# Second-layer experts: all shared blocks first, pairs weighted by ScalarE and summed by TensorE

## The chip, the cores and the metric

The kernel runs on one core of a Trainium2 chip. The metric is the device time of one execution in microseconds (us); the profile is one execution of it, taken by the hardware profiler.

## What is computed

A two-layer network on x of shape 8 x 512 x 128 (float32), with a mixer and a mixture of experts in each layer. The change lies in the last of the four, the experts of the second layer:

```python
xt = x.reshape(-1, D)                                   # 4096 rows of 128
scores = jax.nn.softmax(xt @ gate_w.T, axis=-1)
idx = jax.lax.top_k(scores + gate_b, 2)[1]              # 2 of 8 experts
weights = jnp.take_along_axis(scores, idx, axis=-1)
cw = jnp.sum(jax.nn.one_hot(idx, E) * weights[..., None], axis=1)
h1 = jnp.einsum('td,efd->etf', xt, w1) + b1[:, None, :]
h3 = jnp.einsum('td,efd->etf', xt, w3) + b3[:, None, :]
y = jnp.einsum('etf,edf->etd', swiglu(h1 * h3), w2) + b2[:, None, :]
routed = jnp.einsum('te,etd->td', cw, y)
shared = swiglu((xt @ sw1.T + sb1) * (xt @ sw3.T + sb3)) @ sw2.T + sb2
return routed + shared
```

`swiglu` takes even and odd columns (gate g and lin l), clips them, and gives g * sigmoid(1.702 g) * (l + 1). The result is scaled by `gb` and added to x.

## The kernel before

`program` runs the stages one after another: `prologue`, `scan_phase`, `experts0`, the attention functions, and `experts1` (L1272), which starts near 1500 us with its layer norm and router and works on experts from 1556 us to the end.

**Blocks.** 4096 rows are 32 tiles of 128 (NT). The shared expert works on 16 blocks of 256 rows (SLOTS) taken straight from `hT`. The routed rows are 8192 pairs of row and expert; they are sorted by expert in two parts (PARTS) of 16 tiles each, each part in 23 blocks (RB) of 256 slots, and every block belongs to one expert. VectorE works out where each pair goes (`pos`, L1531 to L1573) and the expert of each block (`eid`, L1580).

**POOL** then issues, with nothing else to do, 64 indirect DMAs that scatter normalized rows to `sorted_h` in HBM (L1440, 32 for each part). For each part it waits until all 23 blocks' results are stored (L1447) and issues 32 indirect DMAs that gather two rows for each row into `got` (L1449); NGOT = 8 semaphores let it run eight tiles ahead.

**SP** loads, for routed block m, 256 rows from `sorted_h` into one of four buffers (`load_slots`, L1400) and 320 KB of weights of the expert `eid[m]`, whose number it reads into a register (`load_weights`, L1391 and L1392), into one of five, and stores y (`store`, L1406). Its loop issues in iteration m: rows of m+1, weights of m, the store of m-5.

**The order of blocks** is a list, ORDER: 11 shared, 46 routed, 5 shared. For block n TensorE turns the rows of block n+1 if it is routed (L1704), does four matmuls of 256 columns (L1717 to L1726: gate and lin products), and the down product of block n-2 (L1741), for a shared block together with the second biases of all nine experts, weighted by `cwT` (L1740). ScalarE adds the first biases (`gate` L1473, `lin` L1479), does tanh (L1485), and copies turned rows (L1467) and y (L1496). VectorE multiplies and clips (L1600 to L1611) and joins (L1617, L1623).

A routed block's first biases are those of its expert. VectorE selects them for all 46 blocks at once in `select_biases`, ahead of its work on block 4.

**Combining.** `acc` holds the shared result of each tile. `combine(k)` adds two gathered rows, each times its weight, with one VectorE operation each that waits for the one before (L1629). Eight tiles of part 0 are combined inside the block loop, every second block, the other 24 after it; `finish(j)` multiplies four tiles by `gb` and adds x (L1635, L1637), and SP stores them (L1421).

## Time and profile before

| | us |
|---|---|
| median of 3 runs | 1889.8 (1887.2 to 1894.68) |
| the profiled execution's own time | 1888.83 |
| its span in the trace | 1887.1 |
| TensorE matmul busy in the span | 1487.2 (79%) |
| VectorE busy | 1326.4 (70%) |
| ScalarE busy | 908.8 (48%) |
| POOL busy | 612.6 (32%) |

In rows of the trace PE is TensorE's matmuls, PEld its weight loads, DVE VectorE, ACT ScalarE, SPq SyncE's queue. A row of the timeline has start, length, engine, line, operation, output and inputs, count, and in brackets the engine's idle time before it and what ended that. "remote" or "another core or an unknown queue" is a semaphore whose writer the trace doesn't tell, "issue" idle time without a visible wait. PEclk is the granted TensorE clock (0.50 is 1.2 GHz, 1.00 is 2.4 GHz). A `pz` is one of the eight PSUM banks; times count from the start of the span.

### The profile page before, as it was taken

To read this page: it belongs to the slowest core of one execution; us is meant where nothing else is said; L and a number is where in the kernel's file an instruction comes from. 1 tells how busy PE (TensorE), PEld (TensorE's weight loads), DVE (VectorE), ACT (ScalarE), POOL (GpSimd) and SP (SyncE) were. 2 spreads that over 40 slices of the span, in tenths; PEclk is the share of its full clock that TensorE was granted. 3 is DMA by queue.
4 is the path that set the end of the run, shared out by engine and by line. 5 is a ranking of instruction groups with operands and counts; after the bars stand their busy time and mean duration, and the time that the engine had idled before them with its cause. 6 is when DMAs were issued, how large, how long until landed. Compare 5 with 4: busy or idle time off the path is not lost. (4 is left out here: it accounts for less than half of the span.)

```text
span 1887.1 us, 41774 instructions
## 1 busy us (share of the span) xinstructions
PE 1487.2 (79%) x15118; PEld 1007.2 (53%) x15118; DVE 1326.4 (70%) x3609; ACT 908.8 (48%) x2099; POOL 612.6 (32%) x586
## 2 busy tenths in 40 slices
PE   1277777767699399999999999999999395298490
PEld 0177766766554245555555555555555363187370
DVE  6699999999559636666666666666666674177385
ACT  1455555555121226666666666666666122065250
POOL 3496666662103325111111111111110317502414
PEclk7688888888789799999999999999999777599695
DMA  1400000000000012111111111111110001258342
GB/s 68 118 12 1 1 1 1 1 1 1 12 1 1 17 17 35 28 29 29 28 29 30 29 29 30 29 30 30 30 25 8 15 1 56 65 150 224 94 135 78
DMA packets 146373, 71.54 MB, mean 38 GB/s; under 512 B 95218, under 2 KB 131588, under 8 KB 146052
## 3 DMA queue, kind: packets, MB, share of 16 engines
q1 hardware_dynamic: 141508, 60.62, 14.6%
q0 software_dynamic: 4096, 8.40, 1.5%
q8 instruction: 107, 1.75, 0.4%
q14 instruction: 86, 0.70, 0.1%
q10 hardware_dynamic: 576, 0.07, 0.0%
HBM read 38.11 MB, written 18.35 MB: 30 GB/s over the span
## 5 line engine op out<-in xcount | busy, mean ns | idle before, releaser
L1190 DVE TENSOR_REDUCE ntop<-score 128x1 f32<-128x512 f32 x512 | 318.1, 683 | 253.0 <-PE score L1071 252.9
L1149 ACT ACTIVATE prob<-score,ntop 128x512 f32<-128x512 f32 x512 | 317.6, 687 | 270.0 <-DVE ntop L1190 269.9
L391 ACT ACTIVATE hist<-zp 128x168 f32<-128x168 f32 (+1 forms) x768 | 224.1, 313 | 171.6 <-DVE zp L359 170.9
L1107 PE MATMUL turned<-ident,prob 128*128 128x128 f32 x2048 | 268.5, 280 | 1.5 <-DVE probT L1133 1.5
L441 PEld LDWEIGHTS py<-hist,diagC 128*128 128x128 f32 x2048 | 262.7, 214 | 0.0
L441 PE MATMUL py<-hist,diagC 128*128 128x128 f32 x2048 | 262.5, 297 | 0.0
L1071 PE MATMUL score<-ks,qs 64*128 64x512 f32 x1024 | 257.5, 622 | 0.0
L1107 PEld LDWEIGHTS turned<-ident,prob 128*128 128x128 f32 x2048 | 218.9, 141 | 49.4 <-issue 28.7
L411 POOL TENSOR_TENSOR xb<-xc,Bm 128x1024 f32<-128x1024 f32 x128 | 244.7, 1950 | 1.3
L354 DVE TENSOR_TENSOR gp<-hist,Ap 128x168 f32<-128x168 f32 (+1 forms) x768 | 231.0, 331 | 14.9 <-POOL xb L411 14.9
L359 DVE TENSOR_TENSOR zp<-gp,xb 128x168 f32<-128x168 f32 (+1 forms) x768 | 234.6, 336 | 0.0
L836 POOL TENSOR_TENSOR qr<-rel_q,own_shift 128x256 f32<-128x256 f32 x64 | 37.2, 613 | 549.3 <-DMA key_q<-q_sb 549.3
L1133 ACT COPY probT<-turned 128x512 f32<-128x512 f32 x384 | 198.4, 594 | 1.2 <-PE turned L1107 1.2
L1071 PEld LDWEIGHTS score<-ks,qs 64*128 64x128 f32 x1024 | 89.1, 188 | 169.0 <-issue 169.0
L1091 PEld LDWEIGHTS mixed<-probT,vh 128*16 128x16 f32 x4096 | 100.7, 96 | 95.8 <-issue 95.8
L1067 PE MATMUL score<-tb,qr 32*32 32x512 f32 x4096 | 148.1, 600 | 4.0 <-PEq L850 3.9
L1091 PE MATMUL mixed<-probT,vh 128*16 128x128 f32 x4096 | 136.4, 274 | 0.7 <-issue 0.7
L1449 POOL DMA_INDIRECT got<-sorted_y,pos x64 | 61.1, 954 | 169.3 <-DMA sorted_y<-ysb 150.4
L1177 DVE RECIPROCAL inv<-cm 128x256 f32<-128x256 f32 x64 | 111.5, 1742 | 0.0
L842 POOL TENSOR_TENSOR qs<-key_q,own_batch 128x256 f32<-128x256 f32 x128 | 95.5, 787 | 0.0
L1133 DVE COPY probT<-turned 128x512 f32<-128x512 f32 x128 | 88.5, 691 | 0.1
L1440 POOL DMA_INDIRECT sorted_h<-hz,pos x64 | 63.2, 987 | 48.9 <-DVE pos L1573 29.7
(299 smaller groups left out, 1652.8 us busy)
## 6 DMA issues: line engine op xcount, KB each, us to landing
w<-in_ew SPq DMA_DIRECT2D x46, 320.0 KB
tb<-in_table SPq DMA_DIRECT2D x64, 127.1 KB
sorted_h<-nought SPq DMA_DIRECT2D x2, 2944.0 KB, 17.1
xs<-sorted_h SPq DMA_DIRECT2D x46, 128.0 KB
sorted_y<-ysb SPq DMA_DIRECT2D x46, 128.0 KB
rel_q<-q_sb SPq DMA_DIRECT2D x256, 8.0 KB
ks<-k_sb SPq DMA_DIRECT2D x32, 128.0 KB
key_q<-q_sb SPq DMA_DIRECT2D x248, 8.0 KB
```

The lines of the kernel that those rows point to most:

```text
L354: v.tensor_tensor(g[:, lo:hi], prev[:, lo:hi], Ap[:, lo:hi], ALU.mult).then_inc(decayed, 1)
L359: v.tensor_tensor(zp[j][:, 0:hi - lo], g[:, lo:hi], xb[:, par, u, lo:hi], ALU.add)\
L391: nc.scalar.activation(hist[:, par, u, lo:hi], zp[j][:, 0:hi - lo], ACT.Tanh)\
L411: nc.gpsimd.tensor_tensor(xb[:, par, u:u + XB_STEPS, :].rearrange("p u (s b) -> p u s b", b=NB), xc[:, par, u * NB:(u + XB_STEPS) * NB].re ...
L441: last = mm(py[par][:, 0:P], diagC[:, s, :], hist[:, par, :, s * NB:(s + 1) * NB], start=False, stop=(s == NS - 1))
L1067: mm(score_ps[r][32 * w:32 * w + 32, :], qr[p][rows, w, g, :, :].rearrange("p b v -> p (b v)"), tb[p][rows, s:s + SEQ], start=True, stop=F ...
L1071: mm(score_ps[r][:, :], qs[p][rows, r % 2, g, :, :, :].rearrange("p w b v -> p (w b v)"), ks[p][rows, :], start=False, stop=True).then_inc ...
L1091: last = mm(mixed_ps[32 * c:32 * c + SUMS, bh * P:(bh + 1) * P], vh[:, p, j, b, :], probT[G // 2 % 2][:, j, :, :].rearrange("p t (w b v) - ...
L1107: last = nc.tensor.transpose(turned_ps[BANK[e]][:, j * P:(j + 1) * P], prob[G % 2][e][:, j * P:(j + 1) * P], ident[:, :])
L1133: copy(probT[G // 2 % 2][:, :, G % 2 * GRP + TURN[e], :], turned_ps[BANK[e]][:, :].rearrange("p (j t) -> p j t", j=JT))\
L1149: nc.scalar.activation(prob[G % 2][e][:, :], score_ps[r][:, :], ACT.Exp, bias=ntop[:, G % 2, e:e + 1]).then_inc(prob_ready, 1)
L1190: v.tensor_reduce(ntop[:, G % 2, e:e + 1], score_ps[r][:, :], AX.X, ALU.max, negate=True)\
```

## The change

It touches `experts1`, and `program` only for sizes that are now lists by part.

- ORDER becomes 16 shared blocks, then 46 routed ones. All shared blocks still add the second biases (`SEEDED` = 16), so the code for later seeding never runs.
- The first biases of the routed blocks are selected by TensorE: `b1_rows` holds the 8 experts' biases with the expert on the partition, `mine` (one VectorE comparison) says which block is whose, four matmuls into XT[0] ahead of block 2 multiply them, and ScalarE copies the result ahead of block 3. `select_biases` goes.
- SP issues the weights of blocks 0 to 4 and the rows of blocks 0 to 5 first (the last two once buffers are free), and in iteration m the weights of m+5, the store of m and the rows of m+6.
- NGOT becomes 4.
- Combining leaves VectorE. After the block loop ScalarE multiplies each gathered row by its weight in place (64 operations on 128x128), TensorE adds the two of a tile into a PSUM bank with the identity (64 matmuls), and VectorE's `finish(j)` adds four tiles' sums to `acc` in one operation ahead of the two that it had. It first waits for all y copies.
- The counting of places runs over quarters of 8 tiles, with three doubling steps and an addition per part; totals come from two small matmuls of their own.

```diff
-    NW, NX, NY, NGOT = 5, 4, 4, 8
+    NW, NX, NY, NGOT = 5, 4, 4, 4
-    SHARED_FIRST, SELECT_AT, IN_LOOP, EVERY = 11, 4, 8, 2
+    SHARED_FIRST, SHARED_THEN = 16, 0
+    SLOTS_AHEAD = NX + 2
+    SEEDED = SHARED_FIRST
+    SELECT_AT = 2
...
@@ sync
-            load_slots(0)
+            for m in range(NW):
+                load_weights(m)
+            for m in range(SLOTS_AHEAD):
+                load_slots(m)
             for m in range(NROUTED):
-                if m + 1 < NROUTED:
-                    load_slots(m + 1)
-                load_weights(m)
-                if m >= AFTER:
-                    store(m - AFTER)
-            for m in range(NROUTED - AFTER, NROUTED):
+                if m + NW < NROUTED:
+                    load_weights(m + NW)
                 store(m)
+                if m + SLOTS_AHEAD < NROUTED:
+                    load_slots(m + SLOTS_AHEAD)
@@ scalar
+                    if n == SELECT_AT + 1:
+                        act.wait_ge(spots_ps, 2)
+                        A.copy(b1_sel[:, :, :].rearrange("p c m -> p (c m)"), XT[0][:, 0:4 * NROUTED])\
+                         .then_inc(sel_ready, 1)
...
+            for k in range(NT):
+                act.wait_ge(got_in[k % NGOT], 32 * ring(k, NGOT))
+                for r in range(2):
+                    A.activation(got[:, 2 * k + r, :], got[:, 2 * k + r, :], ACT.Copy, scale=wt[:, r, k:k + 1])\
+                     .then_inc(weighted, 1)
@@ vector
             for i in range(STEPS):
-                by, dst = 1 << i, upto[(i + 1) % 2][:, :, 1:PT + 1, :]
+                by, dst = 1 << i, upto[i % 2][:, :, :, :]
...
+            for s in range(PARTS):
+                for q in range(T0[s] // QT + 1, T0[s + 1] // QT):
+                    chain.add(v.tensor_tensor(src[:, q, :, :], src[:, q, :, :],
+                                              src[:, q - 1, QT - 1:QT, :].to_broadcast([P, QT, NE1]), ALU.add))
...
+            v.tensor_scalar(mine[:, :], eidf[0:NE1, :], own[0:NE1, 0:1], None, ALU.is_equal).then_inc(eid_ready, 1)
...
-            def combine(k):
-                dve.wait_ge(got_in[k % NGOT], 32 * ring(k, NGOT))
-                for r in range(2):
-                    v.scalar_tensor_tensor(acc[:, k, :], got[:, 2 * k + r, :], wt[:, r, k:k + 1], acc[:, k, :],
-                                           ALU.mult, ALU.add).then_inc(combined, 1)
-                    dve.wait_ge(combined, 2 * k + r + 1)
             def finish(j):
                 ts = slice(j * TPB, (j + 1) * TPB)
+                dve.wait_ge(summed, j + 1)
+                chain(v.tensor_tensor(acc[:, ts, :], acc[:, ts, :],
+                                      pm[SUMS_IN[j]][:, :].rearrange("p (q e) -> p q e", q=TPB), ALU.add))
...
+            dve.wait_ge(y_taken, N)
+            for j in range(NBLK):
+                finish(j)
@@ tensor
+            def select():
+                pe.wait_ge(eid_ready, 2)
+                for c in range(4):
+                    last = mm(XT[0][:, c * NROUTED:(c + 1) * NROUTED],
+                              b1_rows[:, :].rearrange("e (p c) -> e c p", c=4)[:, c, :], mine[:, :],
+                              start=True, stop=True)
+                last.then_inc(spots_ps, 1)
...
+            for j in range(NBLK):
+                if SUMS_IN[j] == 6:
+                    pe.wait_ge(y_taken, N)
+                for q in range(TPB):
+                    k = j * TPB + q
+                    bank = pm[SUMS_IN[j]][:, q * P:(q + 1) * P]
...
+                    for r in range(2):
+                        pe.wait_ge(weighted, 2 * k + r + 1)
+                        last = mm(bank, ident[:, :], got[:, 2 * k + r, :], start=(seeded and r == 0), stop=(r == 1))
+                last.then_inc(summed, 1)
```

## Rows read from the trace of the kernel before

**Rows 1.** Busy time by stretch; columns: stretch, length, then each engine, clock, DMA.

```profile
1568.00:1640.00 72.00, 21.07 (x61) 13.00 (x59) 11.92 (x24) 4.99 (x13) 53.82 (x55) 0.58 0.23 72
...
1661.00:1733.00 72.00, 70.82 (x391) 60.16 (x390) 59.84 (x161) 50.85 (x137) 0.17 (x1) 1.00 0.77 201
1741.00:1778.00 37.00, 5.40 (x14) 3.77 (x14) 2.41 (x6) 2.50 (x8) 23.88 (x26) 0.58 0.29 78
...
1680.00:1700.00 20.00, 19.83 (x111) 16.93 (x110) 17.48 (x47) 14.51 (x40) 0.00 (x0) 1.00 0.86 228
```

**Rows 2.** Waits from 1556 us on: us in total, times, longest.

```profile
ACT acc L1496 <- remote: 72.3, 6, 21.9
...
DVE acc L1629 <- DMA got<-sorted_y,pos: 0.3, 1, 0.3
```

**Rows 3.** ScalarE's timeline in the scatters and after; last row: its gate activations, 1556 to 1640.

```profile
1608.87 0.47 ACT L1479 ACTIVATE l<-pz,b_all 128x256 f32<-128x256 f32 x1 [10.42 <-remote]
1631.27 0.37 ACT L1496 COPY acc<-pz 128x256 f32<-128x256 f32 x1 [21.93 <-remote]
...
1665.36 0.47 ACT L1473 ACTIVATE g<-pz,b_sel 128x256 f32<-128x256 f32 x1 [0.44 <-PE pz L1720]
...
L1473 ACT ACTIVATE g<-pz,b_all x7: 473/474/474, 1557.1 to 1597.7; 128x256 f32<-128x256 f32 x7
```

**Rows 4.** Chain that ended last, 1656 to 1681: gate matmuls of shared, then routed blocks.

```profile
1657.24 0.43 PE pz L1717 x2
...
1660.85 0.43 PE pz L1717 x2
...
1675.29 0.43 PE pz L1717 x2
...
1677.73 0.43 PE pz L1717 x2
```

**Rows 5.** VectorE's timeline in the bias selection.

```profile
1568.07 3.00 DVE L1591 TENSOR_TENSOR b_prod<-done,b_all 128x368 f32<-128x368 f32 x4
1571.11 1.69 DVE L1594 TENSOR_REDUCE b_sel<-b_prod 128x184 f32<-128x1472 f32 x1
```

**Rows 6.** SP's queue in the scatters.

```profile
1606.72 0.00 SPq L1392 DMA_DIRECT2D w<-in_ew  x1
...
1615.82 0.71 SPq L1392 DMA_DIRECT2D w<-in_ew  x1
```

**Rows 7.** Chain, 1785 to 1822: VectorE's gate operations with combining between.

```profile
1788.63 0.50 DVE gg L1600
...
1793.88 0.50 DVE gg L1600
```

**Rows 8.** Chain, 1820 to the end: last y, first gather, one gather's landing.

```profile
1825.59 0.38 ACT ysb L1496
...
1828.52 0.94 POOL got L1449
...
1855.20 2.30 DMA got<-sorted_y,pos
```

**Rows 9.** Timelines at the end: POOL's last gather, ScalarE's last copy, VectorE.

```profile
1867.85 0.94 POOL L1449 DMA_INDIRECT got<-sorted_y,pos  x1 [0.30 <-issue]
...
1873.65 0.37 ACT L1496 COPY acc<-pz 128x256 f32<-128x256 f32 x1 [19.94 <-remote]
...
1860.33 0.35 DVE L1629 SCALAR_TENSOR_TENSOR acc<-got,wt,acc 128x128 f32<-128x128 f32 x1 [1.00 <-DVE acc L1629]
...
1883.98 0.69 DVE L1637 TENSOR_TENSOR x<-x,acc 128x512 f32<-128x512 f32 x1
```

**Rows 10.** Groups of the stage by line; last row: ScalarE's nearest small operation, from the page.

```profile
L1629 DVE SCALAR_TENSOR_TENSOR acc<-got,wt,acc 128x128 f32<-128x128 f32 x64 | 22.5, 351 | 13.6 <-DVE acc L1629 7.3 <-remote 3.6 <-issue 1.0
...
L1449 POOL DMA_INDIRECT got<-sorted_y,pos x64 | 61.1, 954 | 169.3 <-DMA sorted_y<-ysb 150.4 <-issue 18.6 <-DMA got<-sorted_y,pos 0.3
...
L391 ACT ACTIVATE hist<-zp 128x168 f32<-128x168 f32 (+1 forms) x768 | 224.1, 313 | 171.6 <-DVE zp L359 170.9
```

More of the change, by code:

```diff
@@ L41 @@
 NSHARED = NB * SEQ // SLOTS
-RB = 2 * PT * P // SLOTS + NE1 - 1
-NROUTED = PARTS * RB
-MOST = PT * P // SLOTS
+QT = 8
+QUARTERS = NT // QT
+PART_QUARTERS = (2, 2)
+PARTS = len(PART_QUARTERS)
+PT = [QT * q for q in PART_QUARTERS]
+T0 = [sum(PT[:s]) for s in range(PARTS + 1)]
+RB = [2 * t * P // SLOTS + NE1 - 1 for t in PT]
+R0 = [sum(RB[:s]) for s in range(PARTS + 1)]
+NROUTED = R0[PARTS]
+MOST = max(PT) * P // SLOTS
+PART_OF = [s for s in range(PARTS) for _ in range(RB[s])]
 class Chain:
@@ L1279, in experts1 @@
     WCOLS = 5 * P
-    NW, NX, NY, NGOT = 5, 4, 4, 8
+    NW, NX, NY, NGOT = 5, 4, 4, 4
     N = NSHARED + NROUTED
-    AFTER = NW
-    SHARED_FIRST, SELECT_AT, IN_LOOP, EVERY = 11, 4, 8, 2
-    ORDER = ([("shared", i) for i in range(SHARED_FIRST)] + [("routed", m) for m in range(NROUTED)]
-             + [("shared", i) for i in range(SHARED_FIRST, NSHARED)])
+    SHARED_FIRST, SHARED_THEN = 16, 0
+    SLOTS_AHEAD = NX + 2
+    SEEDED = SHARED_FIRST
+    SELECT_AT = 2
+    shared = lambda lo, hi: [("shared", i) for i in range(lo, hi)]
+    routed = lambda lo, hi: [("routed", m) for m in range(lo, hi)]
+    ORDER = (shared(0, SHARED_FIRST) + routed(0, RB[0]) + shared(SHARED_FIRST, SHARED_FIRST + SHARED_THEN)
+             + routed(RB[0], NROUTED) + shared(SHARED_FIRST + SHARED_THEN, NSHARED))
     place_of = {b: n for n, b in enumerate(ORDER)}
@@ L1317, in experts1 @@
         chosen = sb("chosen", [P, NT, NE1])
-        upto = [sb(f"upto{i}", [P, PARTS, PT + 1, NE1]) for i in range(2)]
+        upto = [sb(f"upto{i}", [P, QUARTERS, QT, NE1]) for i in range(2)]
         top = sb("top1", [P, NT])
@@ L1437, in _ @@
             for s in range(PARTS):
-                for k in range(s * PT, (s + 1) * PT):
+                for k in range(T0[s], T0[s + 1]):
                     for r in range(2):
@@ L1443, in _ @@
                 for i in range(NY):
-                    pool.wait_ge(y_out[i], 16 * stores(i, (s + 1) * RB))
-                for k in range(s * PT, (s + 1) * PT):
+                    pool.wait_ge(y_out[i], 16 * stores(i, R0[s + 1]))
+                for k in range(T0[s], T0[s + 1]):
                     if k >= NGOT:
@@ L1525, in _ @@
                                   expn[:, :].unsqueeze(2).to_broadcast([P, NE1, NE1]), ALU.is_lt))
-            for i in range(2):
-                chain.add(v.memset(upto[i][:, :, 0, :], 0.0))
             dve.wait_ge(logits_ready, NBLK)
@@ L1566, in _ @@
             for s in range(PARTS):
[L1567 to L1568 removed]
+                chain.add(v.tensor_tensor(spot[:, T0[s]:T0[s + 1], :], spots[:, T0[s]:T0[s + 1], :],
+                                          base[:, s, :].unsqueeze(1).to_broadcast([P, PT[s], NE1]), ALU.add))
             chain.wait()
@@ L1737, in down @@
                     cols = slice(o * P, (o + 1) * P)
-                    if kind == "shared":
+                    seeded = kind == "shared" and i < SEEDED
+                    if seeded:
                         k = i * HALVES + o
                         mm(Y[n % 2][:, cols], cwT[:, k * P:(k + 1) * P], b2[:, :], start=True, stop=False)
-                    last = mm(Y[n % 2][:, cols], a[:, n % 2, cols], w[:, 4 * P:5 * P],
-                              start=(kind == "routed"), stop=True)
+                    last = mm(Y[n % 2][:, cols], a[:, n % 2, cols], w[:, 4 * P:5 * P], start=not seeded, stop=True)
                 last.then_inc(y_ready, 1)
+            def select():
[3 more added lines that the diff above has]
+                              b1_rows[:, :].rearrange("e (p c) -> e c p", c=4)[:, c, :], mine[:, :],
+                              start=True, stop=True)
+                last.then_inc(spots_ps, 1)
             for n in range(N + 2):
+                if n == SELECT_AT:
+                    select()
+                if n + 1 == SHARED_FIRST:
+                    pe.wait_ge(sel_ready, 1)
                 if n + 1 < N and ORDER[n + 1][0] == "routed":
@@ L1751, in _ @@
                     down(n - 2)
+            for j in range(NBLK):
[4 more added lines that the diff above has]
+                    bank = pm[SUMS_IN[j]][:, q * P:(q + 1) * P]
+                    seeded = k < HALVES * SEEDED
+                    if not seeded:
+                        mm(bank, cwT[:, k * P:(k + 1) * P], b2[:, :], start=True, stop=False)
+                    for r in range(2):
+                        pe.wait_ge(weighted, 2 * k + r + 1)
+                        last = mm(bank, ident[:, :], got[:, 2 * k + r, :], start=(seeded and r == 0), stop=(r == 1))
+                last.then_inc(summed, 1)
 def program(nc, d, out):
-    hs = [nc.dram_tensor(f"sorted_h{s}", (RB * SLOTS, P), F32).ap() for s in range(PARTS)]
-    ys = [nc.dram_tensor(f"sorted_y{s}", (RB * SLOTS, P), F32).ap() for s in range(PARTS)]
+    hs = [nc.dram_tensor(f"sorted_h{s}", (RB[s] * SLOTS, P), F32).ap() for s in range(PARTS)]
+    ys = [nc.dram_tensor(f"sorted_y{s}", (RB[s] * SLOTS, P), F32).ap() for s in range(PARTS)]
     with ExitStack() as ctx:
```

138 lines of the change are left out of this document (59 added, 79 removed).

## The prediction

> **What bounds the kernel now.** I read the stage of the second experts (1556 us to the end, about 331 us) first by busy time per stretch, then by waits, then by the chain. It falls into stretches with different limits [rows 1]. In 1568 to 1640 and 1741 to 1778, TensorE works 21.1 of 72 us and 5.4 of 37 us, at a mean granted clock of 0.58, while POOL issues one indirect DMA after another; and the last such stretch, from 1828.52, decides the end of the kernel. In 1661 to 1733 TensorE is full (70.8 of 72 us) at clock 1.00. So the stage has three stretches with POOL issuing (64 scatters, 32 gathers of part 0, 32 gathers of part 1) and two in which the routed blocks run.
>
> The reader is to see in the waits that the idle time has no plain producer: ScalarE stood 72.3 us "remote" ahead of its copies of shared y [rows 2]. The timeline tells what it looks like [rows 3]: ScalarE's lin activation at 1608.87 stood idle for 10.42 us before it and the copy of y at 1631.27 for 21.93 us, where the gate activation at 1665.36, in the undisturbed stretch, stands idle for 0.44 us. Whatever ScalarE waits for from TensorE comes late while POOL issues; within some 8 us of POOL's last issue it is prompt again. I call this the hold-up. It starts some 8 to 12 us after POOL begins, and its cause is not in the trace.
>
> **The change, part by part.** The sum goes against the profiled execution's own 1888.83 us (span 1887.1); the median of the three runs is 1889.8, inside their spread of 7.5 us, so I add the difference to the median.
>
> 1. Five shared blocks move from the end to the front. Before, they lay under the gathers of part 1 and cost the path nothing. Now they stand between the hold-up of the scatters and the first routed block. A shared block takes 3.61 us from gate matmul to gate matmul at full clock, 1657.24 to 1660.85 [rows 4]; five are 5 x 3.61 = 18.0 us. Could they run inside the scatters' 81 us? Only as far as ScalarE is served there, and that is the hold-up's doing, not the number of blocks'. I take 18.0, and leave what may be gained there to the next term.
>
> 2. The bias selection leaves VectorE. Its products (3.00 us) and their sum (1.69 us) [rows 5] kept VectorE for 4.7 us just as the hold-up began, the comparison ahead of them apart; in their place are four small matmuls with 8 rows and one ScalarE copy at the second and third block, before the hold-up. The gain is what TensorE gets done more before 1570. Since from there ScalarE is served at the hold-up's pace, I take a third of a block, -1.2 us; the bounds are 0 and one whole block, -3.6.
>
> 3. The SP queue: five weight loads now go out as soon as the expert numbers are known (1557), before the scatters hurt, and then rows for four blocks. Before, SP issued the weights of blocks 0 and 1 inside the scatters at 1606.72 and 1615.82, 9.1 us apart with one load of rows and the read of one expert number between [rows 6], those of block 2 likewise, and the fourth and fifth only once block 1 was turned. In the steady loop nothing changes: a load of weights waits for the same y, rows are asked for three blocks ahead as before (blocks m+4 and m+5 wait for turned rows), and a store follows at once instead of in iteration m+5, which comes at the same moment. What is gained is two weight loads of 320 KB that are out of the way when the routed blocks start. The routed blocks are near the transfers' limit: a pure block takes 2.44 us on TensorE, 1675.29 to 1677.73 [rows 4], but 137 ScalarE operations in 72 us at five a block are 27.4 blocks, 2.63 us each [rows 1]. 640 KB at 228 GB/s [rows 1] are 2.8 us; I take -1.5, bounds 0 and -2.8.
>
> 4. VectorE's combining inside the loop goes. In the second routed half VectorE set the pace where it combined: gate operations at 1788.63 and 1793.88, so 5.25 us for two blocks against 4.88 on TensorE [rows 7]. Seven such gaps are 7 x 0.37 = 2.6 us, but the transfers' pace of 2.63 a block is just as slow and may take over. I take -1.0, bounds 0 and -2.6.
>
> 5. The last routed block has no shared block behind it. Before, its down matmuls stood behind the up matmuls of two shared blocks, and its y was copied at 1825.59 [rows 8]; its a would be ready about 0.3 us sooner and the matmuls would follow it at once: -1.5 (0 to -1.7). The prefix sum with three steps instead of four and two small additions: -0.2 (0 to -0.4), since one copy and one addition on 128 columns go. New waits for weights' arrival and the changed constants lie far ahead of their use.
>
> So the last y is copied 18.0 - 1.2 - 1.5 - 1.0 - 1.5 - 0.2 = 12.6 us later (bounds +6.9 and +18.0).
>
> 6. The tail, from the end of that copy (1825.97) to the end of the span (1887.1): 61.1 us now. Its first part stays: first gather at 1828.52, last gather at 1867.85 [rows 8, 9], that is +41.9; landed 2.3 us after its start, a distance that the chain shows for one gather [rows 8], +44.2. What changes is behind that. Now VectorE combines at 0.35 us a piece (64 pieces) [rows 10], during the gathers 1.4 us apart (0.35 at 1860.33 behind 1.00 idle), so that it is behind when they end; it closes the last tiles at 1884.67 [rows 9]. After the change ScalarE weights, TensorE adds with the identity, and VectorE does three operations of 128x512 for four tiles, 3 x 0.69 = 2.1 us [rows 9], in place of 8 x 0.35 + 2 x 0.69 = 4.2 with no pauses [rows 9, 10]. ScalarE's small operation on 128x128 isn't in the trace; the nearest is 128x168 at 0.313 us [rows 10], so I take 0.3, or 0.6 for a tile against 2.5 us between tiles: it keeps up, and part 0's 32 operations (10 us) fit ahead of the hold-up. TensorE's two additions for a tile are 2 x 0.4 us at half clock.
>
> How much the hold-up takes here is the open point. If nothing is late: 44.2 + 0.6 + 0.8 + 2.1 + 2.4 (from the end of x to the span's end, as now) = 50.1. If TensorE's word to VectorE comes as late as its word to ScalarE, the first after the gathers comes at 1873.65 [rows 9], +47.7; with two groups waiting then, 47.7 + 2 x 2.1 + 2.4 = 54.3. If ScalarE too is held at its waits for the gathers and has 12 to 14 tiles left then, 47.7 + 14 x 0.6 + 0.8 + 2.1 + 2.4 = 61.4. I take 54.3, since in the trace the late ones are those that wait for TensorE, while VectorE's wait for gathered rows is 0.3 us in all [rows 2]: -6.8 against 61.1 (bounds -11.0 and +0.3). The ring of four instead of eight makes POOL wait for the gather that lies eight issues (10 us) back, against 2.3 us to land: nothing.
>
> The skill's view of this: the Trainium skill, "SBUF — State Buffer", section "SBUF: two separate sides", says that only the port pair shared by VectorE and GpSimd causes contention and that TensorE and ScalarE never wait on anyone. By that rule the tail would be the 50.1 us, 4.2 less than I take. The rows on ScalarE speak against counting on it, though a late word need not be a port. The same section says that the pair is an exclusive lock, so VectorE's combining (two inputs in SBUF) might slow POOL's gathers; but POOL's first gather took 0.94 us and the mean of all 64 is 0.954 [rows 8, 10], so the whole effect is under 64 x 0.014 = 0.9 us.
>
> **Sum.** +12.6 - 6.8 = +5.8 us: 1888.83 becomes 1894.6, and the median 1889.8 becomes 1895.6. The bounds of all terms together are 6.9 - 11.0 = -4.1 and 18.0 + 0.3 = +18.3: 1885.7 to 1908.1. The front pays for blocks that were free at the end, and the shorter tail gives about half of it back.
>
> **Rivals.** (a) Slower: ScalarE is held in the last gathers. For it speaks that ScalarE alone shows waits of 20 us there; against it that those were waits for TensorE. It decides from about six tiles left at the end of the gathers (each 0.6 us, and the tail comes over 57.9). Its time is 12.6 + 0.3 = +12.9, 1902.7, and up to 1908 with no gain in the terms 2 to 5. (b) Faster: the hold-up isn't a fixed price. VectorE's work inside it goes, SP reads no register inside the scatters, and no block is computed under the last gathers. If the two holds of TensorE's work (72 us of scatters, 37 us of gathers) shrink by a sixth, 18 us go: +5.8 - 18 = -12, 1877.6. For it speaks that SP's own steps were slow just there [rows 6]; against it, that POOL's issuing, which both holds go along with, is unchanged. (c) The front costs nothing: TensorE had room for the five blocks inside the scatters after all, so that they end with it. Then -1.2 - 1.5 - 1.0 - 1.5 - 0.2 - 6.8 = -12.2, 1877.6. Against it: only seven gate activations got through from 1557 to 1640 [rows 3].
>
> **How the numbers follow.** Forecast 1895.6 with 0.58, (a) 0.22, (b) and (c) together 0.20. A measurement tells 0.5%, 9.4 us, from no change: 1880.4 and 1899.2. The forecast's own range, 1885.7 to 1908.1, lies mostly inside that; about a seventh of it over 1899.2. So slower 0.22 + 0.08 = 0.30, faster 0.18, same 0.52. The range reaches down to 1881, where (b) and (c) are left out, and up to 1908.
>
> **What would show it.** Right: first routed gate about 12 to 18 us later than 1661.8; the last y copied near 1838; gathers of part 1 still 1.25 us apart; VectorE's last three-operation group ends 8 to 10 us after the last gather starts to land. Wrong: ScalarE's weightings of part 1 later than 3 us behind their gathers (rival a); more than eight gate activations before 1640, or TensorE busy for over 10 us in the part-0 gathers (b, c). If the hold-up is of another size in this program than in the old one, every term stands on sand: it covers 109 us [rows 1] and most of the last gathers.

## The result and the profile after

| | before | after |
|---|---|---|
| median, us | 1889.8 (1883.4 to 1894.7, 5 runs) | 1904.0 (1902.4 to 1910.0, 5 runs) |
| profiled execution, us | 1888.83 | 1908.53 |
| its span | 1887.1 | 1906.8 |

The ratio is 1.0087, with a 95% interval of 1.0057 to 1.0116: slower by 0.9%, 14.2 us. The forecast was 1895.6, +5.8, and the range of 1881 to 1908 holds the result. So the direction of the sum was right, and it was 8 us too small.

The start of the scatters differs by some us between executions for reasons ahead of the change, so I measure from it. Four marks divide the stage: the first scatter, the gate activation of the first routed block, the end of the last copy of a routed y, and the end of the span.

| us | before | after | difference | forecast |
|---|---|---|---|---|
| span's start to first scatter | 1556.1 | 1554.7 | -1.4 | -0.2 |
| first scatter to first routed gate | 105.7 | 130.8 | +25.1 | +16.8 |
| first routed gate to last y | 164.2 | 162.6 | -1.6 | -4.0 |
| last y to the span's end | 61.1 | 58.7 | -2.4 | -6.8 |
| sum | 1887.1 | 1906.8 | +19.7 | +5.8 |

The profiled execution of after lies 4.5 us over its own median, so the +19.7 of this table is more than the +14.2 of the medians; the rows say where it went, not to the last microsecond how much. How far single executions of the same code differ, the profiles of the experiments below show. In the stretches where they run the code of after, the front took 130.8 us in after, 130.7 in e4 and 136.6 in e3; the routed blocks 162.6 in after, 160.5 in e4, 161.2 in e1 and 164.5 in e5; the tail 58.7 in after, 54.9 in e1 and 55.0 in e5. So only the front's difference is beyond this spread. The front is the loss: more than the whole of it.

Busy time by stretch in after, each stretch moved with its marks from those of [rows 1] (scatters, routed blocks, gathers of part 0); columns as there:

```profile
1567.00:1639.00 72.00, 20.18 (x47) 12.20 (x45) 5.92 (x14) 3.93 (x10) 52.27 (x55) 0.50 0.17 58
1685.00:1757.00 72.00, 69.88 (x385) 59.42 (x385) 59.01 (x160) 51.57 (x136) 0.00 (x0) 1.00 0.73 193
1765.00:1800.00 35.00, 6.91 (x22) 4.54 (x21) 4.23 (x10) 3.15 (x8) 24.37 (x26) 0.58 0.30 84
```

The three stretches look as they did in [rows 1], but in the first TensorE gets 47 matmuls through in place of 61, at a mean clock of 0.50 in place of 0.58. The hold-up is there in both kernels, in scatters and gathers, and the change's program gets less through it. ScalarE's gate activations of after, from the first scatter on, tell the count:

```profile
1556.56 0.47 ACT L1493 ACTIVATE g<-pz,b_shared 128x256 f32<-128x256 f32 x1 [1.29 <-PE pz L1727]
1558.34 0.47 ACT L1493 ACTIVATE g<-pz,b_shared 128x256 f32<-128x256 f32 x1 [0.51 <-PE pz L1727]
1563.39 0.47 ACT L1493 ACTIVATE g<-pz,b_shared 128x256 f32<-128x256 f32 x1 [3.71 <-PE pz L1727]
1578.96 0.47 ACT L1493 ACTIVATE g<-pz,b_shared 128x256 f32<-128x256 f32 x1 [5.04 <-remote]
1610.60 0.37 ACT L1516 COPY acc<-pz 128x256 f32<-128x256 f32 x1 [21.27 <-remote]
1621.80 0.47 ACT L1493 ACTIVATE g<-pz,b_shared 128x256 f32<-128x256 f32 x1 [10.83 <-issue]
...
1681.84 0.47 ACT L1493 ACTIVATE g<-pz,b_shared 128x256 f32<-128x256 f32 x1 [0.44 <-PE pz L1727]
1685.50 0.47 ACT L1493 ACTIVATE g<-pz,b_sel 128x256 f32<-128x256 f32 x1 [0.49 <-issue]
```

Five gates before the last scatter (1634.77) where before had seven [rows 3]. So eleven shared blocks, not four, are left when the scatters are over: seven more, at 3.39 us each (1674.84 to 1678.23 in the same view) 23.7 us. That is the loss of the front: five blocks that the change moved, and two that were not got through.

TensorE and SP's queue in the same stretch (in SP's row the second number is the time from the first to the last of five issues):

```profile
1558.57 0.59 PE L1733 MATMUL pz<-hTz,w_shared 128*128 128x256 f32 x2
1559.10 2.06 PE L1756 MATMUL pz<-mine,b_rows 8*128 8x46 f32 x8
...
1562.49 1.03 PE L1733 MATMUL pz<-hTz,w_shared 128*128 128x256 f32 x2
...
1566.20 1.06 PE L1724 MATMUL pz<-hTz,w_shared 128*128 128x256 f32 x2
...
1556.93 7.81 SPq L1408 DMA_DIRECT2D w<-in_ew  x5
```

The "four small matmuls" of the bias selection are eight instructions and take 2.06 us, more than half a block. At the end of the next block, the third, a pair of matmuls takes 1.03 us instead of 0.59: TensorE has come to the lower clock of 1.2 GHz, and the fourth block runs on it. Neither was in the sum.

The tail: ScalarE's weightings (the first row has 34 of them, for tiles 0 to 16), TensorE's additions (four records for a tile; PEld are its weight loads) and VectorE's groups in the last gathers, of which POOL's last one starts at 1890.40:

```profile
1847.99 10.04 ACT L1539 ACTIVATE got<-got,wt 128x128 f32<-128x128 f32 x34
...
1892.91 0.69 ACT L1539 ACTIVATE got<-got,wt 128x128 f32<-128x128 f32 x2 [1.84 <-DMA got<-sorted_y,pos]
...
1863.36 1.22 PE L1783 MATMUL pz<-got,ident 128*128 128x128 f32 x4 [2.34 <-issue]
...
1878.29 1.22 PE L1783 MATMUL pz<-got,ident 128*128 128x128 f32 x4 [1.07 <-issue]
...
1885.54 0.28 PEld L1783 LDWEIGHTS pz<-got,ident 128*128 128x128 f32 x1 [1.84 <-issue]
1886.94 0.37 PE L1783 MATMUL pz<-got,ident 128*128 128x128 f32 x1 [2.45 <-issue]
1888.35 0.29 PEld L1783 LDWEIGHTS pz<-got,ident 128*128 128x128 f32 x1 [2.52 <-issue]
1889.74 0.37 PE L1783 MATMUL pz<-got,ident 128*128 128x128 f32 x1 [2.43 <-issue]
...
1896.07 3.97 PE L1783 MATMUL pz<-got,ident 128*128 128x128 f32 x17 [0.36 <-issue]
...
1867.88 0.69 DVE L1651 TENSOR_TENSOR acc<-acc,pz 128x512 f32<-128x512 f32 x1 [7.83 <-remote]
...
1896.06 0.69 DVE L1651 TENSOR_TENSOR acc<-acc,pz 128x512 f32<-128x512 f32 x1 [26.04 <-remote]
1898.12 0.68 DVE L1651 TENSOR_TENSOR acc<-acc,pz 128x512 f32<-128x512 f32 x1
...
1903.65 0.69 DVE L1655 TENSOR_TENSOR x<-x,acc 128x512 f32<-128x512 f32 x1
```

ScalarE is never held: each pair of weightings follows its gathers at their own pace, 2.5 us apart, and the last stands 2.5 us behind the start of the last gather. TensorE keeps up until 1882, with tile 25 as the last in time (the row at 1878.29). From 1884 it is held: one record per 2.80 us, then the last 17 in 3.97 us once POOL is done. VectorE gets TensorE's word late from the fourth group on (the row at 1867.88). The additions of tile 19, the last of the fifth group, ended at 1864.6 (the row at 1863.36); VectorE takes that group at 1896.06, 31 us later. The word comes 48.0 us after the last y (47.7 forecast). From there VectorE closes four groups of 2.05 us in a row, where the forecast had two. Only two of the four, the fifth and the sixth, had their sums ready and waited for the word. The seventh and the eighth weren't finished by TensorE before about 1896.4 and 1900.0.

### The profile page after: what moved, and what is told of

Its sections match the earlier page's. It is cut to its first block and busy times, and to the rows that moved or that the text cites. A ratio compares the mean times of both kernels' runs of the same rounds, so it can differ in the third digit from the quotient of the medians.

```text
span 1906.8 us, 42012 instructions
## 1 busy us (share of the span) xinstructions
PE 1519.8 (80%) x15254; PEld 1036.3 (54%) x15254; DVE 1307.4 (69%) x3547; ACT 931.2 (49%) x2164; POOL 612.1 (32%) x587
```

## The experiments

All kernels compute all of the reference's output. Ratios are to the kernel before on the same chip; that one took 1883.6 us beside e1 to e4, 1884.3 beside e5 to e9 and 1878.5 beside e10 to e13, so kernels of different groups are compared by their ratios. Runs e1, e2, e4 and e5 tell apart the parts of the change; e3 and e7 to e13 ask what the hold-up is worth, and what the change is worth without it.

### Weights behind the rows (e1)

```diff
-            for m in range(NW):
-                load_weights(m)
-            for m in range(SLOTS_AHEAD):
-                load_slots(m)
+            for m in range(NX):
+                load_slots(m)
+            for m in range(NW):
+                load_weights(m)
+            for m in range(NX, SLOTS_AHEAD):
+                load_slots(m)
```

> The changed kernel with one thing undone: SyncE asks for the rows of blocks 0 to 3 first (which waits for the first scatters) and for the first five weights after that, as the kernel before did in substance. Theory A (the 1.6 MB of weights that now move beside the first scatters bring the hold-up on two blocks early; 5 gate activations before 1640 us in the changed kernel, 7 before): 7 gate activations before 1640, first routed gate near 1678 instead of 1685.5, time about 7 us under the changed kernel, 1897. Rival B (the two blocks are lost to something else, the bias matmuls or chance): still 5, first routed gate 1685, 1904.

Measured: 1908.5 us (1897.6 to 1911.6, 5 runs), ratio 1.0143 (1.0119 to 1.0167). Five gates in the scatters still. SP's queue in this kernel:

```profile
1592.55 2.40 SPq L1421 DMA_DIRECT2D xs<-sorted_h  x4
1601.98 35.70 SPq L1408 DMA_DIRECT2D w<-in_ew  x5
```

Five weight loads take 35.7 us to issue inside the scatters, against 7.81 us before the hold-up. So the early loads do what the diff says, and they are not by themselves what took two blocks away. The time didn't fall to the 1897 of theory A: the interval of the ratio lies just above that of after, so the early loads aren't the loss.

### Eleven shared blocks first (e2)

```diff
-    SHARED_FIRST, SHARED_THEN = 16, 0
-    SEEDED = SHARED_FIRST
+    SHARED_FIRST, SHARED_THEN = 11, 0
+    SEEDED = NSHARED
```

> The changed kernel with 11 shared blocks first and 5 at the end; all else, the sums by ScalarE and TensorE too, as changed. Both theories: first routed gate 17 us earlier (5 x 3.4), near 1668.5, last routed y near 1831. Theory A (under the last gathers TensorE's words come late, so five blocks there end only some 5 us after the last gather, as before, and all 64 weightings at 0.31 us stand behind them): 1831 + 48 + 20 + 4 = 1903, no gain. Rival B (the blocks get through at their own pace, then weighting follows the gathers): 1831 + 58.7 = 1890.

Measured: 1901.5 us (1898.9 to 1904.8, 4 runs), ratio 1.0099 (1.0072 to 1.0126), which can't be told from after. The first routed gate comes 17 us earlier (1668.6), and the last y at 1834.0, but the five blocks then lie in the last gathers, behind which the sums now wait for TensorE. One of ScalarE's last copies of shared y:

```profile
1864.88 0.37 ACT L1516 COPY acc<-pz 128x256 f32<-128x256 f32 x1 [11.60 <-remote]
```

Of the 17.0 us that the front gives, the tail takes 8.1 (last y to the span's end is 66.8 us here, 58.7 in after) and the routed blocks 2.8; the 6.0 us that are left in the profiled executions don't show in the ratios. So with the sums on ScalarE and TensorE the five blocks cost time at the end too, and by the ratios they are no cheaper there than in front.

### Combining back on VectorE (e4)

ScalarE's 64 weightings, TensorE's 64 additions and VectorE's addition of sums go; VectorE combines behind the block loop:

```diff
+                for k in range(j * TPB, (j + 1) * TPB):
+                    dve.wait_ge(got_in[k % NGOT], 32 * ring(k, NGOT))
+                    for r in range(2):
+                        v.scalar_tensor_tensor(acc[:, k, :], got[:, 2 * k + r, :], wt[:, r, k:k + 1], acc[:, k, :],
+                                               ALU.mult, ALU.add).then_inc(weighted, 1)
+                        dve.wait_ge(weighted, 2 * k + r + 1)
                 finish(j)
```

> The changed kernel with the combining given back to VectorE, two operations a tile, all of it behind the block loop; 16 shared blocks first as changed. It shows what the sums by ScalarE and TensorE are worth by themselves. Theory A (TensorE's word to VectorE is what comes 26 us late at the end; VectorE by itself only slows to 1.4 us a piece): the tail from the last y copy is about 56 us instead of 58.7, time 1902, so the new way of summing brings nothing. Rival B (the sums by ScalarE and TensorE are what made the tail shorter than 61.1): tail 61 or more, time 1906 to 1912.

Measured: 1900.9 us (1894.7 to 1903.0, 4 runs), ratio 1.0100 (1.0077 to 1.0124); after is at 1.0087. Last y (1840.1) to the span's end (1893.0) takes 52.9 us with VectorE and 58.7 with the sums, in one execution each, but no gain shows in the ratios. The sums on two other engines bring nothing that can be measured.

### One gather pair under way (e3)

```diff
-    NW, NX, NY, NGOT = 5, 4, 4, 4
+    NW, NX, NY, NGOT = 5, 4, 4, 1
```

With one semaphore for landed gathers POOL has to wait for each pair before it asks for the next.

> The changed kernel with NGOT = 1: POOL waits for a tile's two gathers to land before it issues the next two, so that a tile takes some 4.2 us instead of 2.5. Theory A (the hold-up comes from transfers of POOL standing in a queue): TensorE works through the gathers of part 0 without a hold (37 us back), the last gathers take 27 us longer, about 1896. Rival B (any indirect DMA of POOL holds up, however sparse): the hold lasts the longer for it, 67 us instead of 37, and the tail 27 us longer, about 1960.

Measured: 1914.3 us (2 runs), ratio 1.0168 (1.0136 to 1.0200). The time is worse, and worse than the 1896 of theory A, but what it is for is in the trace: the stretch of the part-0 gathers, then POOL's issues.

```profile
1760.00:1815.00 55.00, 49.85 (x270) 41.90 (x268) 45.48 (x120) 37.13 (x97) 21.74 (x22) 0.99 0.80 224
...
1770.85 1.02 POOL L1469 DMA_INDIRECT got<-sorted_y,pos  x1 [3.35 <-DMA got<-sorted_y,pos]
1772.17 0.95 POOL L1469 DMA_INDIRECT got<-sorted_y,pos  x1 [0.30 <-issue]
1776.72 1.12 POOL L1469 DMA_INDIRECT got<-sorted_y,pos  x1 [3.61 <-DMA got<-sorted_y,pos]
```

TensorE is busy for 49.85 of 55 us beside the gathers at clock 0.99, where it had 6.91 of 35 us at 0.58 in after. The same gathers, the same bytes, a pause of 3.4 us behind each two: the hold-up is gone. First routed gate (1687.9) to last y (1815.4) takes 127.5 us, not 162.6. What that gains is lost again in the last gathers, which are now POOL's bound at some 4 us a pair (the last at 1899.8): last y to the span's end is 95.1 us.

### Bias matmuls later (e5)

```diff
-    SELECT_AT = 2
+    SELECT_AT = 9
```

> The kernel after with one size changed: the bias matmuls and the selection stand at block 9 instead of block 2, behind the scatters' first half of blocks. Theory A (the eight bias matmuls of 2.06 us each, and the clock that fell to half behind them in the middle of the scatters' stretch, cost two shared blocks there): seven shared blocks' gate activations lie between the first and the last scatter as in the kernel before, not five; the first routed block's gate comes about 2 x 3.4 = 7 us earlier against the first scatter (some 124 us behind it, not 131), and the time is 5 to 9 us under the kernel after: ratio to the kernel before 1.003 to 1.006. Theory B (the place of the biases doesn't matter, the scatters alone set the pace of the blocks beside them, and which of them get through is the chance of the order of loads): still five gates there, first routed gate 129 to 131 us behind the first scatter, ratio 1.008 to 1.012.

Measured: 1908.1 us (1906.8 to 1909.9, 4 runs), ratio 1.0125 (1.0094 to 1.0156). Still five gates; first routed gate 136.0 us behind the first scatter (1552.6 to 1688.6), no sooner than in after and e3 (130.8 and 136.6). (The expectation has 2.06 us for each of the eight matmuls; it is the time of all eight.) TensorE keeps the upper clock through the fourth block here, and then stands idle for 3.06 us:

```profile
1563.39 0.49 PE L1749 MATMUL pz<-w_shared,a 128*128 128x128 f32 x2
1566.94 1.22 PE L1724 MATMUL pz<-hTz,w_shared 128*128 128x256 f32 x2 [3.06 <-issue]
```

So my theory that the bias matmuls and the clock behind them took the two blocks fell. The hold-up starts some 8 to 12 us after the first scatter here as in before and after, whatever TensorE's clock was before it. Weights late with the biases early, and biases late with the weights early, both leave five gates; the two undone together was not run, so which part of the change lets fewer blocks through the hold-up stays open.

### Pairs paced, in the kernel before and in the kernel after (e7, e8)

POOL waits in the scatters for the pair before to land, and in the first 16 pairs of gathers too; the last 16 pairs go as they went. In the kernel after:

```diff
                 for k in range(T0[s], T0[s + 1]):
+                    if k > T0[s]:
+                        pool.wait_ge(scattered[s], 32 * (k - T0[s]))
+                    elif k == T0[s] and s:
+                        pool.wait_ge(scattered[s - 1], 32 * PT[s - 1])
...
+                    if 0 < k < 16:
+                        for i in range(max(0, k - 1), k):
+                            pool.wait_ge(got_in[i % NGOT], 32 * ring(i, NGOT))
```

> The kernel before, with GpSimd waiting before every pair of scatters until the pair before has landed, and the same for the first 16 pairs of gathers; the last 16 pairs of gathers go as before. Theory A (it is the unbroken row of indirect DMAs, one per 1.25 us, that makes the hand-shakes of TensorE, ScalarE and SyncE late; with a pair per 4.05 us that effect is gone): the shared blocks beside the scatters run at about 3.4 to 3.6 us each, so the eleven are done in some 40 us; the first routed block then waits for the first half of the scatters, 16 x 4.05 = 65 us behind the first scatter; the 39 us stretch of gathers in the routed phase no longer stops the blocks, which took 164 us and now take 125 to 135. GpSimd's row becomes the bound in places. Time 1855 to 1879. Theory B (the late hand-shakes come from the rows' DMA traffic or from the memory that they touch, whatever their pace): the blocks stay slow as long as scatters and gathers run, which now is longer by 32 x 1.5 us for the scatters: time 1890 to 1930.

> The kernel after with the same pacing: a pair of scatters, and each of the first 16 pairs of gathers, only when the pair before has landed. Theory A (the change's front costs 24 us only because the scatters hold the blocks up; sixteen shared blocks are 16 x 3.4 = 55 us, and fit beside the first half of the scatters, 65 us): first routed gate 66 to 75 us behind the first scatter instead of 131, routed phase 125 to 145 us instead of 162.6, last 16 pairs of gathers unchanged at 40 us, tail 55 to 59 us. Time 1840 to 1870, ratio 0.974 to 0.99, and no slower than the kernel before paced in the same way. Theory B (the blocks are held up by the traffic itself, or TensorE's clock stays at half in the gaps): first routed gate 100 us or more behind the first scatter, and time 1890 to 1930.

Measured: the kernel before so paced 1846.1 us (2 runs), ratio 0.9798 (0.9760 to 0.9837); the kernel after 1847.9 us (1844.9 to 1852.4, 4 runs), ratio 0.9807 (0.9773 to 0.9842). Both are 2% faster than the kernel before, and they are the same. For the kernel before 1855 to 1879 was expected; it came out 9 us under that. ScalarE's gates beside the scatters in the second of them:

```profile
1586.04 0.47 ACT L1500 ACTIVATE g<-pz,b_shared 128x256 f32<-128x256 f32 x1 [0.49 <-PE pz L1734]
1589.43 0.48 ACT L1500 ACTIVATE g<-pz,b_shared 128x256 f32<-128x256 f32 x1 [0.49 <-PE pz L1734]
```

3.39 us a block, with POOL scattering all along: all sixteen fit beside the first half of the scatters, and the first routed gate comes 71.7 us behind the first scatter (66 to 75 expected for hold-ups by the unbroken row), instead of 130.8. The tail was expected at 55 to 59 us and was 76.5: the first half's gathers, in pairs, were still under way at the last y (1771.4), and POOL's last gather came at 1835.7.

### Paced by two pairs (e9) and by four (e11)

```diff
-                    if k > T0[s]:
+                    if k % 2 == 0 and k > T0[s]:
...
-                    if 0 < k < 16:
-                        for i in range(max(0, k - 1), k):
+                    if k and k % 2 == 0 and k <= 16:
+                        for i in range(max(0, k - 2), k):
```

and with 4 in place of 2.

> The kernel after paced more loosely: GpSimd waits only before every second pair, so that up to four indirect DMAs are under way. Worked out from the loose row (1.25 us per DMA) and one landing of 2.3 us per four, a group takes 4 x 1.25 + 2.3 = 7.3 us, or 1.8 us per DMA against 2.0 in pairs. Theory A (what holds the others up is a row longer than a few DMAs): the blocks run at full pace here too, the scatters take 32 x 3.65 = 117 us instead of 130, and the time is that of pairs within 6 us, rather below it. Theory B (it is the DMAs in flight at once, more than two): the hold-ups are back in part, gates of shared blocks beside the scatters 5 us or more apart, and the time is 10 us or more above that of pairs.

> The kernel after, GpSimd waiting before every fourth pair: eight indirect DMAs in a row. By the rows of the kernel paced by two (a pause of 1.55 us behind each four scatters, 3.4 to 4.4 us behind each four gathers), eight scatters take 11.7 us instead of 12.7, eight gathers 14 instead of 18. Theory A (a row of eight is still short enough): the scatters end 8 us earlier and the gathers of the first half take 56 instead of 70 us; GpSimd is the bound in neither place, so the time is 1800 to 1811. Theory B (the hold-up sets in within the row, with so many under way): blocks beside them slow down again, and the time is 1820 to 1860.

Measured by two: 1811.1 us (1808.3 to 1813.8, 2 runs), ratio 0.9612 (0.9571 to 0.9653). By four: 1839.7 us (1835.6 to 1843.8, 2 runs), ratio 0.9770 (0.9694 to 0.9845). POOL by two, then TensorE beside scatters and beside gathers:

```profile
1583.61 0.96 POOL L1464 DMA_INDIRECT sorted_h<-hz,pos  x1 [1.55 <-DMA sorted_h<-hz,pos]
1584.88 1.05 POOL L1464 DMA_INDIRECT sorted_h<-hz,pos  x1 [0.30 <-issue]
1586.23 0.96 POOL L1464 DMA_INDIRECT sorted_h<-hz,pos  x1 [0.30 <-issue]
1587.49 0.96 POOL L1464 DMA_INDIRECT sorted_h<-hz,pos  x1 [0.31 <-issue]
1590.01 0.96 POOL L1464 DMA_INDIRECT sorted_h<-hz,pos  x1 [1.56 <-DMA sorted_h<-hz,pos]
...
1554.00:1616.00 62.00, 60.57 (x265) 45.54 (x264) 36.77 (x97) 26.95 (x68) 36.53 (x38) 0.92 0.24 77
1688.00:1747.00 59.00, 50.01 (x270) 40.96 (x268) 45.24 (x119) 35.97 (x98) 26.79 (x28) 1.00 0.80 217
```

A pause of 1.55 us behind each four is enough: TensorE is busy for 60.57 of 62 us beside the scatters and 50.01 of 59 us beside the gathers. The scatters take 109.4 us instead of 81.0, and the kernel is some 90 us faster than after. Against pairs the gain is 37 us, where 6 were expected: I had not seen that in pairs POOL's gathers outlast the routed blocks. Of the 41 us between the profiled executions 16.9 lie in the tail, 10.2 in the front, 8.3 in the routed blocks and 6.0 ahead of the first scatter. By four, TensorE beside scatters and beside gathers, then one of ScalarE's rows:

```profile
1554.00:1616.00 62.00, 56.00 (x217) 38.74 (x216) 29.28 (x77) 19.09 (x50) 41.98 (x45) 0.86 0.23 76
1704.00:1754.00 50.00, 36.14 (x182) 28.63 (x180) 28.79 (x75) 22.94 (x62) 31.23 (x32) 0.97 0.69 194
...
1607.22 0.47 ACT L1506 ACTIVATE l<-pz,b_shared 128x256 f32<-128x256 f32 x1 [2.06 <-remote]
```

The late hand-shakes are back, 1 to 4.5 us each instead of 10 to 20: by eight DMAs the hold-up is there, by four all but gone (ScalarE has two such waits beside the scatters of e9, of 1.9 and 1.1 us). What these runs don't separate is the length of the row from the DMAs per us, since both change together: the 64 scatters take 81.0 us unpaced, 92.0 by four pairs, 109.4 by two and 141.6 by one. The number under way at once hardly changes, as one lands 2.3 us behind its start in the unpaced row too [rows 8], where they start 1.25 us apart.

### The scatters alone by two (e13)

The same without the edit in the gathers.

> The kernel after with the scatters alone paced by two, the gathers as they were. It tells the share of the front. Theory A (the change's front is dear because the scatters hold the blocks up, and that is all of what it lost): the first routed gate comes 62 to 66 us behind the first scatter, as with both paced (61.5), not 131; the hold-up of the first gathers stays, and costs the routed blocks the 35 us that it costs now (162.6 instead of 127 us); time 1835 to 1850. Theory B (pacing the gathers was what counted; the front only moves the wait): 1870 or more.

Measured: 1836.3 us (1833.1 to 1839.5, 2 runs), ratio 0.9751 (0.9678 to 0.9825). First routed gate 61.4 us behind the first scatter, from there to the last y 166.5 us. The time is in the range of theory A. In the part-0 gathers, not paced here:

```profile
1692.00:1732.00 40.00, 12.92 (x57) 10.11 (x55) 8.04 (x21) 6.34 (x16) 30.29 (x32) 0.71 0.44 122
```

TensorE is busy for 12.92 of 40 us. Each row of POOL's has its own hold-up, and each goes with its own pacing: by the ratios the one of the scatters is worth some 63 us to the kernel after (1.0087 to 0.9751), that of the first gathers some 26 more (to 0.9612).

### The kernel before, and VectorE's combining, paced by two (e10, e12)

e10 is the kernel before with the pacing by two; e12 is e4 with it.

> The kernel before with GpSimd waiting for the landing of its indirect DMAs before every second pair, in the scatters and in the first 16 pairs of gathers. Set beside the kernel after paced alike (1811.1 us) it gives the price of the whole change without the hold-ups. Theory A (the change lost its time to the hold-ups alone: without them both orders have their shared blocks beside the first half of the scatters, and the routed blocks start when that half has landed): 1805 to 1815 us, equal within 5 us. Theory B (the change costs time of its own, some 10 to 20 us, by sixteen blocks ahead of the first routed one and four groups of sums at the end): 1792 to 1802.

> The kernel after paced by two, with the combining given back to VectorE behind the loop, as in the run that gave it back without pacing. Theory A (sums by ScalarE and TensorE bring nothing; the last gathers set the end, and VectorE keeps up with them in 0.6 us per half pair): the tail behind the last y is 52 to 56 us instead of 59.6, time 1803 to 1808. Theory B (behind a loop that ends earlier VectorE has all 32 pairs left, 32 x 1.4 = 45 us, and is done later than the sums were): 1811 to 1820.

Measured: e10 1807.1 us (1805.2 to 1808.6, 4 runs), ratio 0.9598 (0.9543 to 0.9653); e12 1810.6 us (1807.6 to 1813.6, 4 runs), ratio 0.9610 (0.9555 to 0.9664). With e9 at 0.9612 all three are the same within their intervals: the change is worth nothing that can be measured once the scatters and the first gathers are paced, with its new way of summing or without it. (The new way of summing with eleven shared blocks first was not run paced.) The tail of e12 was 59.3 us, where 52 to 56 was expected. The four marks of the profiled executions:

| us | before | after | before by two (e10) | after by two (e9) |
|---|---|---|---|---|
| to the first scatter | 1556.1 | 1554.7 | 1550.0 | 1549.7 |
| to the first routed gate | 105.7 | 130.8 | 60.9 | 61.5 |
| to the last y | 164.2 | 162.6 | 133.2 | 135.8 |
| to the span's end | 61.1 | 58.7 | 59.9 | 59.6 |
| span | 1887.1 | 1906.8 | 1804.0 | 1806.6 |

The front's +25.1 has become +0.6: the first routed block waits for the first half of the scatters, and sixteen blocks are done by then as eleven are. The tail is a row of gathers in all four, and no way of summing shortens it. In e10, POOL's last gather and VectorE's last combining, which waits for gathers alone:

```profile
1793.13 0.94 POOL L1456 DMA_INDIRECT got<-sorted_y,pos  x1 [0.31 <-issue]
...
1795.76 0.74 DVE L1636 SCALAR_TENSOR_TENSOR acc<-got,wt,acc 128x128 f32<-128x128 f32 x2 [1.70 <-DMA got<-sorted_y,pos]
```

e10 has the lowest ratio of the study, though e9 and e12 can't be told from it: 4% faster than the kernel before, by nothing but a wait in front of every second pair.

## Why the prediction came out as it did

**Term 1, five blocks to the front: right, and mis-sized.** 18.0 us were five blocks at 3.61. They cost 5 x 3.39 = 17.0 (the 3.61 had 0.22 us for turning a routed block's rows in it), and two more blocks had to be done behind the scatters, 6.8 us. That what the scatters' stretch lets through is "the hold-up's doing, not the number of blocks'" held: with eleven first it is five blocks too (e2). The step that failed is the assumption behind the sum, that the hold-up lets seven blocks through in either program. The prediction ended by saying that every term stands on sand if the hold-up is of another size in the new program; that is what happened. Why it was of another size isn't settled (e1, e5).

**Term 2, bias selection: wrong.** It was a gain of 1.2 us with a bound at zero. The matmuls, called small, take 2.06 us, and the clock falls to 1.2 GHz soon after them. Taken to block 9 they leave the time where it was (e5), so the term is about nothing, but the bound at zero wasn't justified by a row.

**Terms 3 to 5, 4.0 us in the routed blocks: 1.6 came,** which is inside the spread of single executions (160.5 to 164.5 us with this code). The weights are early, and the chain of after has no load of weights in the routed blocks, where that of before has three, of 3.4 to 4.1 us. But it has eight loads of rows instead, of 3.3 to 4.4 us. One of them:

```profile
1708.37 3.73 DMA xs<-sorted_h
```

That is the case named in term 4, that the transfers' pace takes over.

**Term 6, the tail: -2.4 instead of -6.8.** The time of VectorE's word was right, 48.0 against 47.7 us, and so were the two groups waiting for it. The step that failed is that TensorE's own work was left out of the hold-up, at 0.8 us behind the last weighting: from 1884 TensorE was held itself, the sums of two more groups came only at about 1896.4 and 1900.0, and VectorE closed four groups behind the word, 8.3 us instead of 4.2. That is so in this execution, and not in every one of this code. In e1 TensorE kept up with the gathers to the end, and two groups were left:

```profile
1887.28 1.22 PE L1785 MATMUL pz<-got,ident 128*128 128x128 f32 x4 [1.34 <-ACT got L1541]
...
1889.21 0.69 DVE L1653 TENSOR_TENSOR acc<-acc,pz 128x512 f32<-128x512 f32 x1 [18.61 <-PE pz L1785]
1891.27 0.68 DVE L1653 TENSOR_TENSOR acc<-acc,pz 128x512 f32<-128x512 f32 x1
```

The tail was 54.9 us there and 55.0 in e5, against 54.3 in the forecast. What decides whether TensorE is held in this row stays open.

**The rule of the ports.** The Trainium skill, "SBUF — State Buffer", section "SBUF: two separate sides", has TensorE and ScalarE wait on no one for SBUF. By that rule the tail would have been 50.1 us; the traces have 58.7 in after and 54.9 in e1. In after there are 2.4 us of idle time ahead of each record of TensorE's near the end, and ScalarE's waits in the scatters last up to 21.27 us. The rule is about ports, and no run here says that a port is what they wait for; but as a guide to what a stage takes it doesn't hold in these rows, and in e9 and e10, beside the paced row, it does.

**Rivals.** (a), ScalarE held in the last gathers: its time, 1902.7, was nearest to the result, and its mechanism is refuted. ScalarE's weightings kept 2.4 to 3.1 us behind the start of the later of their two gathers; it was TensorE that was held, and the larger part came from the front. (Its threshold doesn't come out of the prediction's own sum either: 47.7 + 0.8 + 2.1 + 2.4 and 0.6 a tile pass 57.9 at about eight tiles, not six.) (b) and (c), faster by room in the hold-up: refuted in this program; (c) is true of the paced kernels, where the front costs 0.6 us. The misses of the profiled execution are 8.3 us at the front, 2.4 in the routed blocks and 4.4 in the tail, less 1.2 for the earlier start: the 13.9 between +19.7 and +5.8.

**Range and chances.** The upper bound of 1908.1 was made of terms at their bounds. The result came near it through two lost blocks, 6.8 us, that no term had; that it lay inside is partly luck.

## What to carry to other kernels

Where two engines' hand-shakes come late as long as a third issues DMAs in a row, look at that row first, before moving work around it: here a wait for landing after every four indirect DMAs took 4% off a kernel from which reordering had taken nothing. Pacing costs the issuing engine time (81 us for 64 scatters unpaced, some 110 by every second pair), so pace only rows with other work beside them, and as loosely as the trace allows: by two DMAs POOL became the bound, by eight the hold-up was back. And a block moved "to where it is free" is free only against a bound that stays the same; read off how many blocks the place lets through, and what changes that.

## What was not expected of the hardware

An unbroken row of indirect DMAs of 128 rows, one per 1.25 us, holds up the steps of TensorE, ScalarE, VectorE and SP from some 8 to 12 us after its start, and on the whole longer the longer it runs: 1.8, 5.6, 13.7, 10.8, 9.9 and 21.9 us for successive waits of ScalarE in e5. SP's queue is held too: five weight loads of 320 KB take 35.7 us to issue inside the row (e1) and 7.8 at its start (after). The sum of the bytes is not the cause: with the same DMAs paced, TensorE is busy for 60.57 of 62 us, and all queues together move more per us (77 against 58 GB/s in the scatters, 217 against 84 in the gathers).

Most of what is late is a word from engine to engine. Waits for landed DMAs end on time (ScalarE's weightings in after, VectorE's combining in e10). But it isn't only that. In the tail of after TensorE's weight loads and matmuls follow each other 1.40 us apart (1885.54, 1886.94, 1888.35, 1889.74), though one addition of the program is two loads and two matmuls and has one wait, ahead of the first. And in the last gathers of before VectorE stands idle for 1.00 us behind its own operation [rows 9], where in e10 two of them take 0.74 us together. Nor is every engine held alike, or in every execution. In the last gathers, unpaced here too, TensorE is held in after and e11 and not in e1, e5, e8, e9 and e13. In e9 it follows ScalarE tile by tile to the end, and VectorE alone gets its word late:

```profile
1794.33 1.22 PE L1790 MATMUL pz<-got,ident 128*128 128x128 f32 x4 [1.27 <-ACT got L1546]
...
1799.98 0.69 DVE L1658 TENSOR_TENSOR acc<-acc,pz 128x512 f32<-128x512 f32 x1 [13.46 <-remote]
```

All traces here are recorded ones, and the times too come from profiled executions, so whether the recording has a part in the hold-up can't be told from these runs. That would be the first thing to try next, and after it a pause behind every sixth DMA.
